# A fused attention and MLP kernel on one core: other lead-in, weights prepared mid-stage, es transposes moved behind the third q/k tile

## The reference, cut to what matters

```python
xn = layernorm(x)
q, k = rope(xn @ Wq.T), rope(xn @ Wk.T)            # 16 heads x 128
v, g = xn @ Wv.T, xn @ Wg.T
s = clip(xn @ Ws1.T @ Ws2.T + bs2, -32, 32)        # 16 heads x 64 slots, rank 16
es, enz = exp(s), exp(-cumlogsumexp(s))            # over the tokens
ok = enz * (tril(q k^T) * scale) @ es
qv = softmax(ok)                                   # over the 64 slots
o = tril((qv * enz) @ es^T) @ v
attn = (o * rsqrt(mean(o*o) + eps) * g_norm * silu(g)) @ Wo.T
gate, up, down = dequantised 4-bit codes * scales
mlp = (gelu(xn @ gate.T) * (xn @ up.T)) @ down.T
out = x + attn + mlp
```

## Time and profile before

| | us |
|---|---|
| median of 3 runs (range) | 1124.58 (1122.58 to 1124.82) |
| the profiled execution, its own time | 1122.49 |
| its span, first to last instruction | 1120.0 |
| PE busy | 1084.0 (97%) |
| DVE busy | 928.1 (83%) |
| ACT busy | 650.6 (58%) |
| POOL busy | 425.5 (38%) |
| mean granted TensorE clock | 0.985 |

### The profile page before, as it was taken

One profiled execution on the slowest core, in us unless ns is written; L12 is line 12 of the kernel. 1 busy time (PEld: TensorE's weight loads), 2 busy tenths in 40 slices (PEclk: granted clock), 3 DMA queues, 4 the chain that ended last, 5 costly groups with the idle time before them and its releaser, 6 DMA issues.

```text
span 1120.0 us, 20624 instructions
## 1 busy us (share of the span) xinstructions
PE 1084.0 (97%) x7176; PEld 927.7 (83%) x7176; DVE 928.1 (83%) x1687; ACT 650.6 (58%) x2103; POOL 425.5 (38%) x308
## 2 busy tenths in 40 slices
PE   6888999999999999999999999999999999999996
PEld 5677888888888888888888888888888888888875
DVE  6788889888888889888888888888888898888863
ACT  4465566655655657555666656565665556655542
POOL 7142245432524345232453324443252334523231
PEclk9899999999999999999999999999999999999996
DMA  4002000020002000020000200011000200000001
GB/s 166 1 1 78 1 2 1 2 77 1 1 1 78 1 2 1 1 78 1 1 1 1 78 1 2 1 38 41 1 1 1 78 1 1 1 1 20 1 20 38
DMA packets 9526, 23.06 MB, mean 21 GB/s; under 512 B 848, under 2 KB 5840, under 8 KB 8528
## 3 DMA queue, kind: packets, MB, share of 16 engines
q1 hardware_dynamic: 9424, 21.76, 5.4%
HBM read 19.66 MB, written 2.10 MB: 19 GB/s over the span
## 4 chain that ended last, share of the span: by engine, by line
PE 84%; DVE 7%; issue 4%; POOL 2%; ACT 2%; DMA 0%; POOLq 0%; DVEq 0%; ACTq 0%
PE bank L205 20%; PE bank L207 19%; PE bank L206 19%; PE bank L303 4%; PE bank L366 4%; PE bank L316 3%; PE bank L337 3%; DVE xs L930 2%; PE bank L375 2%; PE bank L305 2%; PE bank L328 1%; PE bank L529 1%; PE bank L346 1%; PE bank L319 1%; PE bank L359 1%
## 5 line engine op out<-in xcount | busy, mean ns | idle before, releaser
L1200 POOL TENSOR_TENSOR inter_lo<-ffb,inter_hi 128x512 fp32r<-128x512 f32 x64 | 83.3, 1325 | 440.5 <-ACT inter_hi L678 440.5
L1191 POOL TENSOR_TENSOR qkT<-ra,xs 128x512 f32<-128x512 f32 x128 | 170.2, 1329 | 109.6 <-DVE xs L930 80.8
L640 ACT ACTIVATE sm<-bank,mx 128x64 f32<-128x64 f32 x256 | 76.5, 326 | 120.6 <-DVE mx L886 120.6
L930 DVE TENSOR_TENSOR xs<-xs,rope 128x512 f32<-128x512 f32 x128 | 129.5, 1012 | 0.0
L927 DVE TENSOR_TENSOR ra<-bank,rope 128x512 f32<-128x512 f32 x128 | 87.7, 685 | 46.9 <-ACT xs L622 44.7
L621 ACT ACTIVATE xs<-bank 64x512 f32<-64x512 f32 x128 | 76.2, 595 | 66.8 <-PE bank L207 43.8
L205 PE MATMUL bank<-xh,wqk_hi 128*128 128x512 f32 x256 | 109.9, 429 | 3.1 <-DVE h L990 2.6
L875 DVE RECIPROCAL enzT<-enzT 128x256 f32<-128x256 f32 x64 | 111.4, 1742 | 0.0
L205 PE MATMUL bank<-xh,wgu_hi 128*128 128x512 f32 x256 | 105.6, 412 | 0.0
L645 ACT ACTIVATE At<-bank 128x128 f32<-128x128 f32 x128 | 35.8, 281 | 114.1 <-DVE At L809 112.9
L205 PE MATMUL bank<-wvg_hi,xh 128*128 128x512 f32 x256 | 101.1, 395 | 1.0 <-DVE xl L978 1.0
(11 more groups left out here) (149 smaller groups left out, 3075.5 us busy)
## 6 DMA issues: line engine op xcount, KB each, us to landing
raw<-in_w_qkvg SPq DMA_DIRECT2D x7, 1024.0 KB, 5.0
scaled<-in_w_scaled SPq DMA_DIRECT2D x8, 640.0 KB, 7.1
packed<-in_w_packed SPq DMA_DIRECT2D x8, 384.0 KB, 5.7
acc<-in_x SPq DMA_DIRECT2D x4, 512.0 KB, 8.1
out<-acc SPq DMA_DIRECT2D x3, 512.0 KB, 2.9
raw<-in_w_qkvg SPq DMA_DIRECT2D x2, 512.0 KB, 7.1
out<-acc SPq DMA_DIRECT2D x2, 256.0 KB, 2.1
ws_raw<-in_w_slot SPq DMA_DIRECT2D x8, 48.0 KB, 1.8
```

Source lines behind the costliest of these rows:

```text
L640: ins = act.activation(sm[:, c], src[:, c], ACT.Exp, bias=mx[:, g:g + 1], accum_out=ssum[:, g:g + 1])
L930: dve.tensor_tensor(two(xs[i % 2][:, :]), two(xs[i % 2][:, :]), sin, ALU.mult).then_inc(sin_done, 1)
L1191: pool.tensor_tensor(qkT[:, i, :], ra[i % 2][:, :], xs[i % 2][:, :], ALU.add).then_inc(roped, 1)
L1200: pool.tensor_tensor(inter[1][e][:, :], ffb[e][:, :], inter[0][e][:, :].bitcast(F32), ALU.subtract).then_inc(inter_lo, 1)
```

## The change

It has three parts.

The lead-in and stages 0 and 1. x of pair 1 is loaded ahead of the slot and MLP weights and normalised ahead of most of the decoding; its two transposes come one behind the other into two banks, ahead of q/k tiles 2 and 3, and its rank-16 product ahead of stage 0. x of pairs 2 and 3 is scaled by ACT (`x_scale_act`, with a bias from DVE's small `x_bias`) and no longer by DVE; own small tiles (`xvar`, `xrs`, `xnb`) hold its statistics. `x_stats(2)` stands ahead of stage 0. In stages 0 and 1 `transpose_x(prep, 0)` stands behind `outputs` 0 and `project_vg` 2, directly ahead of `slot_rows`. In stage 0 `softmax_in` stands ahead of `cumulate(1, 1)`.

The weights of the next head pair. The codes are the first of the DMAs. `decode` 0 and 1 stand in the middle of bp = 1, 2 to 4 in the middle of bp = 2. `prepare_scales` goes to bp = 2, `prepare_out` to bp = 0 of its own head pair. `split_hi` of W_QK and W_GU and `split_lo` of W_GU stand in the first two thirds of bp = 3.

The es transposes. `project_qk` 2 stands ahead of `slot_transpose`, which comes directly ahead of `slot_weights`; ACT's `copy_J` stands directly ahead of `swap_halves` 2.

```diff
@@ SP @@
             load_x(0)
             sp.dma_start(raw_k[:, :, 512:1024], first[:, :, 512:1024]).then_inc(raw0_in, 16)
             sp.dma_start(raw_k[:, :, 0:512], first[:, :, 0:512]).then_inc(raw_in, 16)
+            load_x(1)
             sp.dma_start(ws1, w_slot1).then_inc(ws1_in, 16)
...
-            load_x(1)
...
+                sp.dma_start(packed[:, :], w_packed[hp + 1]).then_inc(packed_in, 16)
                 sp.dma_start(ws2_raw[:, :], w_slot[hp + 1]).then_inc(ws2_in, 16)
                 sp.dma_start(raw[:, :], w_qkvg[hp + 1]).then_inc(raw_in, 16)
-                sp.dma_start(packed[:, :], w_packed[hp + 1]).then_inc(packed_in, 16)
@@ PE, lead-in @@
             transpose_x(1, 0, rg[1])
+            transpose_x(1, 1, sc[0])
             project_qk(0, 0, 0, 2)
             project_qk(0, 0, 0, 3)
+            pe.wait_ge(h1_done, 2)
+            pe.wait_ge(h1_lo, 1)
+            slot_scores(None, 0, 0)
+            slot_inner(1, sc[1])
@@ PE, stage @@
                 if first:
                     mlp_up(st, bp, hp, 0)
-                    x_split(KT + 1)
-                    transpose_x(1, 1, rg[1])
                     mlp_up(st, bp, hp, 1)
                 for i in (0, 1):
+                    if first and i == 1:
+                        pe.wait_ge(h1_done, 4)
+                        pe.wait_ge(h1_lo, 2)
...
                     scores(st, bp, i, hp)
                 if first:
-                    pe.wait_ge(h1_done, 2)
-                    pe.wait_ge(h1_lo, 1)
-                    slot_scores(None, 0, 0)
                     mlp_up(st, bp, hp, 2)
-                    slot_inner(1, rg[1])
...
-                    pe.wait_ge(h1_done, 4)
-                    pe.wait_ge(h1_lo, 2)
...
                 slot_states(st, bp)
+                if not first:
+                    outputs(st, 0, php, None)
+                if not last:
+                    project_vg(st + 1, nbp, nhp, 2, True)
                 if prep:
                     pe.wait_ge(clip_done, st + 2)
                     transpose_x(prep, 0, sc[0])
-                if not first:
-                    outputs(st, 0, php, None)
-                if not last:
-                    project_vg(st + 1, nbp, nhp, 2, True)
                 slot_rows(st)
...
                 if not last:
                     project_qk(st + 1, nbp, nhp, 1)
+                if not last:
+                    project_qk(st + 1, nbp, nhp, 2)
                 pe.wait_ge(qe_ready, st + 1)
...
-                if not last:
-                    project_qk(st + 1, nbp, nhp, 2)
                 slot_weights(st, bp)
@@ ACT @@
+            def x_scale_act(bp):
+                act.wait_ge(xnb_done, bp - 1)
+                if bp == 3:
+                    act.wait_ge(xT_full, KT * bp)
+                for i in range(NT):
+                    ins = act.activation(xn[bp][:, i, :], acc[:, bp * NT + i, :], ACT.Identity,
+                                         bias=xnb[:, i:i + 1], scale=xrs[:, i:i + 1])
+                ins.then_inc(xn_act, 1)
...
+            swap_halves(0, 0)
             swap_halves(0, 1)
+            split_hi(0, W_GU)
             x_hi(1, 0, rg[1])
+            x_hi(1, 1, sc[0])
             swap_halves(0, 2)
             swap_halves(0, 3)
-            x_hi(1, 1, rg[1])
+            inner_copy(1, sc[1])
...
+                if bp == 0 and not first:
+                    prepare_out(hp)
+                if bp == 2 and more:
+                    prepare_scales(hp + 1)
                 if bp == 3 and more:
                     split_hi(hp + 1, W_VG)
                 off_diagonal(st, 2)
+                if bp == 3 and more:
+                    split_hi(hp + 1, W_QK)
                 off_diagonal(st, 3)
                 gate_square(st, 1)
+                if first:
+                    x_scale_act(prep)
...
                 copy_state(st)
+                if bp == 3 and more:
+                    split_hi(hp + 1, W_GU)
+                if st == 1:
+                    x_scale_act(prep)
...
-                if bp == 3 and more:
-                    split_hi(hp + 1, W_QK)
-                    prepare_scales(hp + 1)
-                    prepare_out(hp + 1)
...
                     swap_halves(st + 1, 1)
-                    copy_J(st + 1, rg[1][:, :])
-                if bp == 3 and more:
-                    split_hi(hp + 1, W_GU)
                 if bp == 2 and more:
                     split_slot(hp + 1)
                 if not last:
+                    copy_J(st + 1, rg[1][:, :])
                     swap_halves(st + 1, 2)
@@ DVE, lead-in @@
-            for part in range(5):
-                decode(0, part)
+            x_stats(1)
+            decode(0, 0)
+            decode(0, 1)
+            x_scale(1)
+            gate_g(0, 0, 0)
+            gate_g(0, 0, 1)
+            decode(0, 2)
+            decode(0, 3)
+            decode(0, 4)
+            gate_g(0, 0, 2)
+            gate_g(0, 0, 3)
             slot_lo(0)
-            for i in range(NT):
-                gate_g(0, 0, i)
-            x_stats(1)
...
+            inner_lo(0, rg[0])
             rope_cos(0, 0)
             rope_sin(0, 0)
-            x_scale(1)
             rope_cos(0, 1)
             rope_sin(0, 1)
-            inner_lo(0, rg[0])
             x_lo(1, 0, rg[1])
+            x_lo(1, 1, sc[0])
             rope_cos(0, 2)
             rope_sin(0, 2)
-            x_lo(1, 1, rg[1])
             rope_cos(0, 3)
             rope_sin(0, 3)
+            inner_lo(1, sc[1])
+            x_stats(2)
@@ DVE, stage @@
-                if prep:
+                if st == 1:
                     x_stats(prep)
...
-                if prep:
-                    x_scale(prep)
+                if st == 1:
+                    x_bias(prep)
...
+                softmax_in(st, par)
+                if first:
                     cumulate(1, 1)
-                softmax_in(st, par)
...
+                if bp == 2 and more:
+                    decode(hp + 1, 2)
+                    decode(hp + 1, 3)
                 softmax_max(st)
...
+                if bp == 1 and more:
+                    decode(hp + 1, 0)
+                    decode(hp + 1, 1)
                 if bp == 2 and more:
-                    decode(hp + 1, 2)
-                if bp == 3 and more:
                     decode(hp + 1, 4)
...
-                if bp == 1 and more:
-                    decode(hp + 1, 1)
-                if bp == 2 and more:
-                    decode(hp + 1, 3)
@@ POOL @@
             split_lo(0, W_QK)
+            x_pow(1)
...
             dequantise(0, W_GU)
-            x_pow(1)
+            rotate(0, 0)
             split_lo(0, W_GU)
-            for i in range(4):
+            for i in range(1, 4):
                 rotate(0, i)
+            x_pow(2)
...
                 if bp == 3 and more:
                     dequantise(hp + 1, W_GU)
+                    split_lo(hp + 1, W_GU)
                 hidden_lo(st, 0)
                 hidden_lo(st, 1)
                 if not last:
                     for i in range(4):
                         rotate(st + 1, i)
-                        if i == 1 and bp == 3 and more:
-                            split_lo(hp + 1, W_GU)
```

More of the change, by code:

```diff
@@ L124, in build @@
         mv = sb("mv", [P, NT, 2])
+        xvar = sb("xvar", [P, NT])
+        xrs = sb("xrs", [P, NT])
+        xnb = sb("xnb", [P, NT])
         bank = [ctx.enter_context(nc.psum_tensor(f"bank{i}", [P, 512], F32)) for i in range(8)]
@@ L168, in build @@
             sem("roped"), sem("inter_lo"), sem("pow_done"), sem("w_lo"))
+        xnb_done, xn_act = sem("xnb_done"), sem("xn_act")
         ident_set, raw0_in, vg0_hi, vg0_lo = sem("ident_set"), sem("raw0_in"), sem("vg0_hi"), sem("vg0_lo")
@@ L420, in transpose_x @@
             def transpose_x(bp, k, dst):
-                pe.wait_ge(xn_done, bp + 1)
+                if bp < 2:
+                    pe.wait_ge(xn_done, bp + 1)
+                else:
+                    pe.wait_ge(xn_act, bp - 1)
                 for i in range(NT):
@@ L509, in stage @@
                 slot_states(st, bp)
-                if prep:
-                    pe.wait_ge(clip_done, st + 2)
-                    transpose_x(prep, 0, sc[0])
                 if not first:
@@ L516, in stage @@
                     project_vg(st + 1, nbp, nhp, 2, True)
+                if prep:
+                    pe.wait_ge(clip_done, st + 2)
+                    transpose_x(prep, 0, sc[0])
                 slot_rows(st)
@@ L700, in _ @@
             ins.then_inc(ws1_hi, 1)
-            prepare_scales(0)
             copy_v(0, 0, 0)
             copy_v(0, 0, 1)
+            prepare_scales(0)
             split_slot(0)
@@ L706, in _ @@
             copy_v(0, 0, 3)
-            split_hi(0, W_GU)
-            swap_halves(0, 0)
             act.wait_ge(const_set, 4)
             inner_copy(0, rg[0])
+            swap_halves(0, 0)
             swap_halves(0, 1)
+            split_hi(0, W_GU)
             x_hi(1, 0, rg[1])
```

(33 more changed lines are left out.)

## The result

| | before | after |
|---|---|---|
| median (range) of the runs side by side | 1124.37 (1122.58 to 1124.82) | 1107.72 (1106.81 to 1108.13) |
| the profiled execution's own time | 1122.49 | 1107.82 |
| its span | 1120.0 | 1105.5 |
| stage 0 begins | 36.7 | 31.4 |
| stage 1 begins | 74.4 | 66.7 |

Times in us. A stage begins with its first `scores`. The ratio is 0.9854, interval 0.9837 to 0.9871: 16.6 us faster by the medians, 14.7 by the profiled executions. Of the 14.5 us between the two spans, 7.7 lie ahead of stage 1, 1.6 in stage 1 and 5.6 in the 29 stages 2 to 30; the last stage is 0.3 longer (48.0 for 47.7).

The account below looks back on a forecast made before the run. PE is busy throughout settled stages, leaving lead-in, stages 0 and 1 and bp = 0 to win. 3.7 + 0 + 2.2 + 7.2 - 2.5 = 10.6 us off: 1111.9 profiled, median 1114.0 (1124.6 - 10.6), range 1108.5 to 1120.5.

Parts of the forecast that it names:

- bp = 0: Seven stages with bp = 0 after the first: their whole excess goes, 0.53 each, 3.7 us (bounds 1.5 and 4.2).
- The decodes, costed at nothing: Five moved decodes only change place inside DVE's time: cost nothing, a slipped one its own length, under 1 us.
- The es transposes: In 31 stages, `carried` is not late for `copy_J`, by 0.15 us: cost zero, bounds 1 us saved or lost.
- Stage 1: PE's waits in stage 1 fall from 4.0 to 1.8 us: gain 2.2 (bounds 1.0 and 3.0).
- Lead-in and stage 0: From 19 us on, losses fall from 17.6 to 10.4: gain 7.2 us, less 2.5 for one clock fall (bounds 0 and 6).
- its 17.6: Lead-in and stage 0 of the kernel before: PE's waits of 13.6 us plus clock losses of 4.0.
- The median taken 2.1 above the profiled execution: Whole kernel: the median of the runs lies 2.1 us above the profiled execution, so the forecast starts from 1124.6.
- The parts named for that end (13.1, 0.8, 0.5 and 1): Range's lower end, 16.1 us off: no clock fall, upper bounds of stage 1 and bp = 0, another 1 us of waits.
- The slower one: Rival, 31 stages: `carried` waits for `copy_J` beyond the 0.15 us slack, 14 us, giving 1128.0; chance 0.05.
- The scans: Rival, seven stages: a `cumulate` scan is caught behind POOL's moved split, about 0.9 each, 6.3 us, giving 1120.3; chance 0.06.
- "The clock stays up": Rival, lead-in and stage 0: waits of up to 2.1 us each don't lower the clock; 13.1 off, 1111.5; chance 0.22.
- a sign that the prediction had set against itself: Ahead of 75 us: a clock below 1.00 in more than one stretch would show the prediction wrong.

Follow-up runs that it names:

- e4: The kernel before with only the next head pair's weights prepared mid-stage: 1119.84 us, ratio 0.9969.
- e1: The kernel before with the mid-stage weights and the moved es transposes, without the new lead-in: 1114.67 us, ratio 0.9921.
- e3: The kernel before with only the es transposes (and `copy_J`) moved: 1118.94 us, ratio 0.9963.
- T: The edit that moves the es transposes behind `project_qk` 2, and `copy_J` with them; alone on the kernel before (e3) 1118.94 us.
- e2: The changed kernel with the es transposes back between q/k tiles 1 and 2 and `copy_J` as before: 1110.15 us, ratio 0.9888.
- e11: The changed kernel with 34 more matmuls, output unused, in PE's waits of the last stage alone: 1101.74 us, ratio 0.9807.
- e8: The changed kernel with a second, unread copy of esJ on ACT ahead of the real one, in all stages but the first: 1120.18 us, ratio 0.9975.
- e5: The changed kernel with 15 more matmuls, output unused, in PE's waits of stage 0 alone: 1105.69 us.
- e12: The changed kernel with unused matmuls in stage 0 (15) and the last stage (34), and `inner_lo` of pair 3 earlier in stage 1: 1100.86 us, ratio 0.9800.
- e9: The changed kernel run once more, unedited, as the measure for runs beside it: 1107.11 us.

## Why the prediction missed

Against the profiled execution the sum was 10.6 us and 14.7 were measured. Two terms of the sum failed: the lead-in with stage 0, whose waits and clock cost were put too high (4.7 us of gain forecast, 7.7 measured), and the move of the es transposes, put at zero with bounds of 1 us (at least 1.6 measured). Point by point:

- **bp = 0: 3.7 forecast, 3.9 measured** (six stages 0.51 over the others, one 0.79). e4 shows it alone: 4.0 over its 29 stages. Place and time of the split and the room on ACT were right. The decodes, costed at nothing, were not free in stage 1: `qe` is 0.9 late in e4, and `inner_lo` 0.8 later in e1 than in e3. T covers the first in the changed kernel, the second is still there.
- **The es transposes: 0 forecast with bounds of 1 us; 1.6 measured in the settled stages alone, and 2.4 to 5.2 between medians of whole kernels.** The step that failed reads: "Cost zero. The bounds: PE saves at most the 0.03 of one change of operand form". The 0.03 is there, but 0.054 are gained, and the saving was taken as an end of the range when it was a sure term: a settled stage is 32.91 without T (before, e2, e4) and 32.85 with it (e1, after, and e3 where no split is in the way). And the move was weighed in settled stages only. In stage 1 it puts a q/k tile ahead of two late operands, 1.6 us between e2 and after; in this account those stand in the stage 1 term. With 1.6 in the sum and the bounds moved by it, the range would have held the time.
- **Stage 1: 2.2 forecast, 1.6 measured** (39.5 to 38.0). The wait of the second transposes was 1.0 as forecast, that for `inner_lo` 1.1 and not 0.5, which is the whole difference; the decodes moved ahead of it cover that (0.8 from e3 to e1).
- **Lead-in and stage 0: 7.2 less 2.5 for the clock, 4.7 forecast; 7.7 measured** (stage 1 begins at 66.7 for 74.4). This term failed by the largest amount, 3.0 of the 4.1 us. Each wait forecast was found, but they sum to 7.4 us in this execution, not 10.4, and the fall cost little. The two terms were counted beside one another where they overlap: at half speed PE arrives late and finds less to wait for. Where the clock stayed up (e11, same instructions in stage 0) the waits are 8.6 us and stage 1 begins at 65.8. So the waits were put 1.8 too high, and this fall cost 0.95 net, not 2.5. The two come to 3.4 where 3.0 were missing. The 0.4 between them lies on the side of the kernel before: its 17.6 less 8.6 make 9.0, and from 74.4 to 65.8 are 8.6. Which part of the 17.6 was too much is open.
- **The median taken 2.1 above the profiled execution.** The three runs shown had 1124.58; 35 runs have 1122.9. That offset was no property of the kernel: after has its profiled execution 0.1 above its median. Falls that lay otherwise in those runs are its likely cause, which isn't shown. It decides whether the time lies in the range: the lower end stood for 16.1 us off, and 14.7 were measured between the profiled executions. The parts named for that end (13.1, 0.8, 0.5 and 1) come to 15.4, not 16.1.
- **The rivals.** The slower one did not come, with the slack as worked out, 0.15; e8 and e3 show that it was real. The scans met POOL, but in `dequantise`, at 0.31 us for a pair and with nothing waiting. The first of the pair took 1.00 us in place of 0.68, 0.32 more; it began 0.45 before `dequantise` ended. The Trainium skill, SBUF — State Buffer, "Who interferes with whom", has a two-input instruction of DVE and a reading one of GpSimd exclude each other for a whole instruction. A scan held up for 0.32 of the 0.45 us that POOL's instruction had left agrees with that in the main. "The clock stays up" came in the profiled executions of e5, e11 and e12 before the last stage, and not in after or e9. e9 had two low stretches ahead of 75 us, a sign that the prediction had set against itself.

## What to carry to other kernels

A saving per stage that is small but certain, times the number of stages, belongs in the sum, not in the bounds; and a moved instruction is to be read in the odd stages too, where it may cover a wait. Waits and a lower clock in the same stretch are one loss, not two: work out the stretch at full clock with its waits, then add only what PE at half speed exceeds the other engines' chain by. When a kernel has waits of some us near its start or end, try unused matmuls in them: here 34 of them made the last stage 3.9 to 5.3 us shorter. And when falls differ from one execution to the next, compare the same stages of two profiles and not only medians.

## What the runs showed of the hardware

- The clock falls are not fixed by the program. After, e9 and e11 have the same instructions up to stage 31; one had a low stretch at 49.4 (6.8 us), one at 28.5 and 52.4 (3.4 and 6.8 us), one none. Runs of one kernel spread over 3.2 us with falls (e9), and over 0.5 to 1.0 us with next to none (e11, e12, granted clock 0.998 to 1.000).
- Waits of 2.1 and 1.8 us were enough for a fall in some executions and not in others, and behind a wait of 1.9 in stage 1 one came in e1, e3 and e4 (at 90.9, 91.7 and 93.0), where before has the same wait and no fall. The Trainium skill, TensorE: Matmul & The Clock Gate, "Why this matters for your kernels", ties a fall to one long gap; no gap near the fall at 49.4 is over 1.8 us.
- A fall of 6.8 us with PE busy for 5.15 cost 0.95 us where other engines held PE up as well (after against e11, start of stage 1).
- A scan that began 0.45 us before POOL's `dequantise` ended took 1.00 us in place of 0.68, in six of the seven stages with bp = 3; in the seventh it began 0.27 before the end and took 0.83.
